# Layer norms moved into the stages around them, with their statistics taken block by block and a sqrt issued on ScalarE at a stage's end

## What is computed

```python
x = x + softmax_attention(_layernorm(x))
x = x + spline_ffn(_layernorm(x))
x = x + retention(_layernorm(x))
x = x + spline_ffn(_layernorm(x))
x = x + linear_attention(_layernorm(x))
x = x + conv_attention_moe(_layernorm(x))
x = x + rwkv(_layernorm(x))
x = x + conv_attention_moe(_layernorm(x))
```

```python
y = _layernorm(x)                       # of the layer's input
h = conv3(_layernorm(y) * ln1_w + ln1_b)  # causal, 3 taps, per channel
y = y + softmax_attention(h)            # with rope, 16 heads of 8
y = y + moe(_layernorm(y) * ln2_w + ln2_b)  # 4 experts, top 1
x = x + y
```

## Time and profile before

| | us |
|---|---|
| median of 3 runs | 2646.72 (2646.5 to 2649.6) |
| the profiled execution, device time | 2643.61 |
| its span in the trace | 2641.8 |
| PE, DVE, ACT, POOL busy | 2139.3, 1833.2, 1376.9, 362.9 |
| mean granted PE clock | 0.915 of 2.4 GHz |

### The profile page before, as it was taken

How to read it: one execution, slowest core, us unless ns; L and a number is a source line. 1 busy time by engine, 2 the same in 40 slices (tenths; PEclk the granted TensorE clock), 3 DMA queues, 4 the chain that set the end, 5 groups by cost and what they waited for, 6 DMA issues and landing times. The chain is left out here.

```text
span 2641.8 us, 39751 instructions
## 1 busy us (share of the span) xinstructions
PE 2139.3 (81%) x13146; PEld 943.1 (36%) x13324; DVE 1833.2 (69%) x4630; ACT 1376.9 (52%) x1968; POOL 362.9 (14%) x608
## 2 busy tenths in 40 slices
PE   3689999946799736557999998998347999999898
PEld 2123332224344424422233323665222233322565
DVE  6688788656577766668878874334968888884433
ACT  3246666772599643333566666222533566667221
POOL 4000110010454304100001001000000001101000
PEclk8699999987899868769999999999669999999899
DMA  7501020001011000061011000000052010000000
GB/s 193 140 1 37 2 38 1 1 1 48 31 51 45 18 0 1 0 189 36 1 38 38 1 1 1 1 0 0 0 163 61 1 38 21 18 1 1 1 0 16
DMA packets 48073, 81.68 MB, mean 31 GB/s; under 512 B 6348, under 2 KB 37836, under 8 KB 47228
## 3 DMA queue, kind: packets, MB, share of 16 engines
q1 hardware_dynamic: 42408, 71.34, 10.7%
q0 software_dynamic: 2528, 5.65, 0.7%
q10 hardware_dynamic: 2976, 2.67, 0.4%
HBM read 56.18 MB, written 23.07 MB: 30 GB/s over the span
## 5 line engine op out<-in xcount | busy, mean ns | idle before, releaser
L854 ACT ACTIVATE probs<-score 128x1024 f32<-128x1024 f32 x960 | 825.5, 896 | 522.8 <-PE score L918 519.7
L976 DVE TENSOR_REDUCE max_part<-stat 128x1 f32<-128x512 f32 x1152 | 722.0, 683 | 113.0 <-PE stat L868 110.4
L931 PE MATMUL pv<-probs,v_ones 128*9 128x512 f32 (+3 forms) x3840 | 443.7, 534 | 2.2 <-issue 1.0
L973 DVE CUSTOM_DVE_ANT_0 masked_scores<-stat,mask_row 128x128 f32<-128x128 f32 (+3 forms) x768 | 343.1, 487 | 102.2 <-PE stat L868 98.9
L868 PE MATMUL stat<-first_group_k,first_group_q 128*128 128x512 bf16 (+3 forms) x924 | 293.2, 371 | 91.1 <-DVE max_part L976 37.1
L828 POOL TENSOR_SCALAR_AFFINE_SELECT probs<-probs 128x256 f32<-128x256 f32 x384 | 154.0, 406 | 1249.3 <-ACT probs L854 1245.9
L868 PE MATMUL stat<-group_k,group_q 128*128 128x512 bf16 (+3 forms) x933 | 281.2, 348 | 18.3 <-DVE max_part L976 9.8
L918 PE MATMUL score<-first_group_q,first_group_k 128*128 128x512 bf16 (+3 forms) x921 | 253.3, 355 | 14.7 <-DMA first_group_q<-row_max_turned 8.3
L918 PE MATMUL score<-group_q,group_k 128*128 128x512 bf16 (+3 forms) x915 | 244.8, 348 | 10.1 <-DMA group_q<-row_max_turned 3.5
L1952 ACT ACTIVATE gate<-gate_ps 128x512 f32<-128x512 f32 x128 | 76.4, 597 | 262.0 <-PE gate_ps L1927 262.0
L868 PEld LDWEIGHTS stat<-first_group_k,first_group_q 128*128 128x128 bf16 x960 | 94.0, 99 | 269.3 <-DVE max_part L976 123.4
(11 more groups left out here) (308 smaller groups left out, 2353.9 us busy)
## 6 DMA issues: line engine op xcount, KB each, us to landing
q_parts<-parts_t SPq DMA_DIRECT2D x40, 384.0 KB, 4.0
group_k<-k_parts SPq DMA_DIRECT2D x18, 384.0 KB
group_q<-q_parts SPq DMA_DIRECT2D x18, 384.0 KB
k_parts<-parts_t SPq DMA_DIRECT2D x16, 384.0 KB, 4.9
head_q<-q_parts SPq DMA_DIRECT2D x48, 96.0 KB
head_k<-k_parts SPq DMA_DIRECT2D x48, 96.0 KB
first_group_k<-k_parts SPq DMA_DIRECT2D x9, 384.0 KB
first_group_q<-q_parts SPq DMA_DIRECT2D x9, 384.0 KB
```

The lines of the kernel that those rows point to most:

```text
L854: nc.scalar.activation(probs[:, n % PSLOTS, :, 0:width], sc[hp][:, :, 0:width], ACT.Exp, scale=scale).then_inc(expd.sem, 1)
L931: last = nc.tensor.matmul(acc[32 * h:32 * h + D + 1, f:BANK], v9[:, kt, g * HG + h, :], probs[:, (2 * t + h // 2) % PSLOTS, h % 2, 0:BANK ...
L973: nc.vector.tensor_tensor_reduce(masked[:, at % 2, 0:width], ring[n % RBANKS][:, 0:width], w["mask_row"][:, BANK - width:BANK], 1.0, NEG, ...
L976: nc.vector.reduce_max(into, ring[n % RBANKS][:], AX.X).then_inc(stat_used.sem, 1)
```

## The change

Every `layer_norm` stage and both `conv_stage`s go. What they did is spread over the stage before and the stage behind.

- **Statistics.** `RowStats.follow` is called behind each block's add in `output_stage`, `spline_ffn_stage` and `rwkv_stage`; it takes the statistics of the block before and gathers those of the block before that. What is left comes behind the last add. `experts_stage` takes them in `block_stats`, inside its loop. Only the first norm, of the loaded input, takes them all at once, as before (`known=False`).
- **Norm.** `Norm.dve`, `Norm.act` and `Norm.turn` stand at the head of the stage that uses the norm. Of each block DVE now normalises three tiles and ACT one, and ACT copies all four transposed blocks. PE transposes blocks 0 and 1, and the others between its own matmuls.
- **Double norm.** The two norms of conv_attention_moe's input are one pass: the variance of a normalised row is var / (var + eps), so the second scale follows from the first variance. The result of the first norm, `y`, is written by ACT later in `qkv_stage` (`first_norm`). The convolution runs by block on DVE (`convolve`): two blocks in the norm, two in front of `prepare` of the loop.
- **A root at the end.** `load_roots` takes the square root of one column of zeros as ACT's last instruction of a stage; nothing reads it.
- `output_stage` writes one PSUM bank for each block and adds 512 columns in one DVE instruction (before 128). `project_stage` has four PSUM banks (before eight).
- `EARLY` is 2 instead of 3: ACT reads back the rows of block 1, SP those of block 0, and the attention stage loads blocks 2 and 3.
- POOL's add of a bias, or of `y`, to `X` now waits until all rows are normalised.

```diff
-EARLY = 3
+EARLY = 2
...
+class RowStats:
...
+    def take(self, q):
+        for i in range(QC * q, QC * q + QC):
+            ins = self.nc.vector.bn_stats(self.raw[:, i, :], self.src[:, i, :])
+        ins.then_inc(self.read.sem, 1)
+    def gather(self, dve, q):
+        dve.wait_ge(self.read.sem, self.read.at(q + 1))
+        for i in range(QC * q, QC * q + QC):
+            ins = self.nc.vector.bn_aggr(self.mv[:, i, :], self.raw[:, i, :])
+        ins.then_inc(self.ready.sem, 1)
...
+    def follow(self, dve, q, rows):
+        if q >= 1:
+            dve.wait_ge(rows.sem, rows.at(q))
+            self.take(q - 1)
+        if q >= 2:
+            self.gather(dve, q - 2)
+        if q == NQ - 1:
+            dve.wait_ge(rows.sem, rows.at(NQ))
+            self.take(NQ - 1)
+            self.gather(dve, NQ - 2)
+            self.gather(dve, NQ - 1)
...
+def load_roots(k, w):
+    k.nc.scalar.sqrt(w["root"][:], w["mask_row"][:, 0:1])
...
+class Norm:
...
+        if not self.known:
+            for i in range(NT):
+                ins = nc.vector.bn_stats(self.raw[:, i, :], self.src[:, i, :])
+            chain(ins)
+            for i in range(NT):
+                ins = nc.vector.bn_aggr(mv[:, i, :], self.raw[:, i, :])
+            chain(ins)
+        ins = nc.vector.tensor_scalar(std[:, 0], mv[:, :, 1], self.eps, None, ALU.add)
+        if self.twice:
+            chain(ins)
+            ins = nc.vector.scalar_tensor_tensor(std[:, 1], std[:, 0], self.eps, mv[:, :, 1], ALU.mult, ALU.add)
+        ins.then_inc(self.var_ready.sem, 1)
+        if between:
+            between()
...
+        dve.wait_ge(self.std_ready.sem, self.std_ready.at(1))
+        chain(nc.vector.reciprocal(rstd[:], std[:]))
+        nc.vector.scalar_tensor_tensor(self.shift[:], bcast(mv[:, :, 0], 1, self.N), -1.0, rstd[:], ALU.mult, ALU.mult).then_inc(self.scale_ready.sem, 1)
+        for n, q in enumerate(self.order):
+            for i in range(QC * q, QC * q + QC - 1):
+                ins = nc.vector.tensor_scalar(self.dst[:, i, :], self.src[:, i, :], mv[:, i, 0:1], rstd[:, self.N - 1, i:i + 1], ALU.subtract, ALU.mult)
...
+            ins.then_inc(self.dve_rows.sem, 1)
+            if hook:
+                hook(n)
+        self.steps = chain.n
+    def act_tile(self, out, which, i):
...
+        nc = self.nc
+        act.wait_ge(self.var_ready.sem, self.var_ready.at(1))
+        nc.scalar.sqrt(self.std[:], self.std[:]).then_inc(self.std_ready.sem, 1)
+        act.wait_ge(self.scale_ready.sem, self.scale_ready.at(1))
...
+        def row(n):
+            self.act_tile(self.dst, self.N - 1, QC * self.order[n] + QC - 1).then_inc(self.act_rows.sem, 1)
+        row(0)
+        for n, q in enumerate(self.order):
+            if n + 1 < NQ:
+                row(n + 1)
+            act.wait_ge(self.turned.sem, self.turned.at(n + 1))
+            out = self.dst_t[:, q * BANK:(q + 1) * BANK]
+            if self.affine is None:
+                ins = nc.scalar.copy(out, self.banks[n])
+            else:
+                ins = nc.scalar.activation(out, self.banks[n], ACT.Identity, bias=self.affine[1][:, 0:1], scale=self.affine[0][:, 0:1])
+            ins.then_inc(self.kept.sem, 1)
...
+    def first_norm(self, out, c):
+        for i in range(QC * c, QC * c + QC):
+            ins = self.act_tile(out, 0, i)
+        ins.then_inc(self.first_out.sem, 1)
...
+    def convolve(self, dve, q):
...
+        here = self.conv[:, at:at + BANK]
+        dve.wait_ge(self.kept.sem, self.kept.at(q + 1))
...
+        ins.then_inc(self.convolved.sem, 1)
...
+    def turn(self, pe, n):
+        q = self.order[n]
+        pe.wait_ge(self.dve_rows.sem, self.dve_rows.at(n + 1))
+        pe.wait_ge(self.act_rows.sem, self.act_rows.at(n + 1))
+        for i in range(QC):
+            ins = self.nc.tensor.transpose(self.banks[n][:, i * P:(i + 1) * P], self.dst[:, QC * q + i, :], self.w["ident"][:])
+        ins.then_inc(self.turned.sem, 1)
+    def wait(self, eng, n):
+        sig = self.kept if self.conv is None else self.convolved
+        eng.wait_ge(sig.sem, sig.at(n + 1))
...
                 for q in range(NQ):
                     for n in range(q * NP, q * NP + NP):
@@ -402,53 +482,68 @@
                 for n, (_, dst) in enumerate(units):
                     act.wait_ge(turned.sem, turned.at(n + 1))
                     nc.scalar.copy(dst, tp[:, n % 4, :]).then_inc(kept.sem, 1)
+                load_roots(k, w)
...
-                    nc.vector.tensor_tensor(x[:, i, :], out[:, i % 4, 0:C], x[:, i, :], ALU.add).then_inc(used.sem, 1)
+                for q in range(NQ):
+                    dve.wait_ge(ready.sem, ready.at(q + 1))
+                    tiles = x[:, QC * q:QC * q + QC, :]
+                    nc.vector.tensor_tensor(tiles, out[:, q, :].rearrange("p (i c) -> p i c", c=C), tiles, ALU.add).then_inc(used.sem, 1)
+                    stats.follow(dve, q, used)
...
+                    norm.wait(pe, c)
...
+                    if c == 1:
+                        norm.wait(pe, NQ - 1)
...
+                norm.turn(pe, 0)
+                norm.turn(pe, 1)
                 project(0)
+                norm.turn(pe, 2)
+                norm.turn(pe, 3)
                 project(1)
...
+                norm.act(act)
...
+                    if norm.twice:
+                        norm.first_norm(first_norm, n)
                 if rows:
-                    load_rows(act, EARLY - 1)
+                    load_rows(act, 1)
...
+                def conv_ahead(n):
+                    if norm.conv is not None and n >= 2:
+                        norm.convolve(dve, n - 2)
+                norm.dve(dve, hook=conv_ahead)
...
                 prepare(0, lambda: None)
                 for n in range(NQ):
+                    if norm.conv is not None and n + 2 < NQ:
+                        norm.convolve(dve, n + 2)
...
-                    if rows and 0 < c < EARLY:
-                        load_rows(sp, c - 1)
+                    if rows and c == 1:
+                        load_rows(sp, 0)
...
                     for half in range(2):
+                        norm.turn(pe, 2 * c + half)
+                    for half in range(2):
+                        norm.wait(pe, 2 * c + half)
...
+                norm.act(act)
...
+                load_roots(k, w)
             @block.gpsimd
             def _(pool):
+                norm.wait_read(pool)
                 nc.gpsimd.tensor_tensor(x[:], x[:], bcast(w["bout"][:], 1, NT), ALU.add).then_inc(biased.sem, 1)
...
+                norm.dve(dve)
...
+                norm.turn(pe, 0)
+                norm.turn(pe, 1)
...
+                        if n == 0:
+                            if q + 2 < NQ:
+                                norm.turn(pe, q + 2)
+                            norm.wait(pe, q)
...
                 nc.scalar.activation(wa[:, 0, :], w["wT"][:, 8, :], ACT.Copy, scale=w["mix"][:, 0:1]).then_inc(wa_ready.sem, 1)
+                norm.act(act)
                 nc.scalar.activation(wneg[:], w["decay"][:], ACT.Exp).then_inc(w_ready.sem, 1)
...
+                load_roots(k, w)
...
-                chain(nc.vector.tensor_scalar(om[:], w["mix"][:], -1.0, 1.0, ALU.mult, ALU.add))
-                for n in range(3):
-                    nc.vector.tensor_scalar(wb[:, n, :], w["wT"][:, 8 + n, :], om[:, n:n + 1], None, ALU.mult).then_inc(wb_ready.sem, 1)
+                    stats.follow(dve, q, added)
+                def mix_weights():
+                    chain(nc.vector.tensor_scalar(om[:], w["mix"][:], -1.0, 1.0, ALU.mult, ALU.add))
+                    for n in range(3):
+                        nc.vector.tensor_scalar(wb[:, n, :], w["wT"][:, 8 + n, :], om[:, n:n + 1], None, ALU.mult).then_inc(wb_ready.sem, 1)
+                norm.dve(dve, between=mix_weights)
...
+                norm.turn(pe, 0)
+                norm.turn(pe, 1)
                 for i in range(NT):
+                    if i % QC == 0:
+                        if i // QC + 2 < NQ:
+                            norm.turn(pe, i // QC + 2)
+                        norm.wait(pe, i // QC)
                     ins = nc.tensor.matmul(lp[:, i * E:(i + 1) * E], h_t[:, i * P:(i + 1) * P], w["router"][:], start=True, stop=True)
...
+                norm.wait_read(pool)
                 nc.gpsimd.tensor_tensor(x[:], x[:], y[:], ALU.add).then_inc(added.sem, 1)
...
+                norm.act(act)
...
+                load_roots(k, w)
...
+                norm.dve(dve)
...
+                    if e < 0:
+                        block_stats(n)
+                def block_stats(n):
+                    tiles = [n * QC - QC + s for s in range(QC)]
+                    dve.wait_ge(out_used.sem, out_used.at(n * (E * QC)))
+                    for i in tiles:
+                        xi = x[:, bass.ds(i, 1), :].rearrange("p o c -> p (o c)")
+                        ins = nc.vector.bn_stats(w["row_stats"][:, bass.ds(i, 1), :].rearrange("p o s -> p (o s)"), xi)
```

(8 more changed lines are left out.)

256 lines of the change are left out of this document (117 added, 139 removed).

## The result

The changed kernel took 2635.0 us (median of 6 runs, 2623.8 to 2637.0), the kernel before 2648.5 beside it; forecast were 2609.7 and a range from 2599 to 2621. The ratio is 0.9936 (95% interval 0.9923 to 0.9950): 17 us faster by the ratio (13.5 between the two medians), where 37 were forecast and 26 to 48 were the range. A second set gave 2629.8 against 2647.1, ratio 0.9927 (0.9910 to 0.9943). The profiled execution took 2623.8 us, 19.8 less than the profiled one before. It is the shortest of its kernel, so I take lengths of stretches from it, and not the total. The direction was right and the forecast more than twice too large.

What follows compares the result with a forecast made beforehand. Norms were taken as bound by latency: DVE, ACT and PE work in turn, none full, awaiting all 16 tiles. Terms summed to 37.05 us, taking the profiled 2643.6 to 2606.6 and the median 2646.7 to 2609.7; range 2599 to 2621.

Steps and rivals of the forecast that it cites:

- Roots: Norm roots and their table: cost 0, since `load_roots` puts the table load ahead of the eps operation.
- rival 3: Root's table loaded again at eps: 11 roots, up to 1.1 us each, 12 in all; gain 25, 2622; chance 0.07.
- Statistics: Behind a stage's last add: shorter wait to eps, gain about 1.15 us at spline 1, 3.15 at rwkv; last experts stage loses 1.2.
- Norm in the stage: At the head of the stage using it: PE's own work begins 3.6 us after eps starts instead of 6.6.
- Experts: Start of the two experts stages, up to the logits: gain 1.0 us each with statistics, 2.0 together.
- rival 2: Cold starts: PE at half clock behind every transpose; gain 29.5 us, kernel 2617; chance 0.22.
- Double norm to rope: Convolution layers, from first norm's eps to first rope instruction: 14.75 us instead of 27.67, gain 12.9.
- minus 3.5 (range 2.5 to 4): Convolution layers' DVE-bound loop: loss from two of four blocks' convolutions now inside it, 2 x 1.5 us and their waits.
- The read-back: Two early blocks: convolution layers' stage end gains 2.8 us (1.5 to 4); late attention reads lose 0.8 for both layers.
- The +0.8 of landing: Attention 1: a gain of 0.8 us from landing, part of that layer's 3.0.
- rwkv: Scan start 10.75 us after eps instead of 9.11: loses 1.65; with 3.15 from statistics, gains 1.5.
- rival 4: Slower: lower PE clock in the long attention loops; a mean fall of 0.02 gives 2656 us; chance 0.03.

Runs made afterwards that it cites:

- e4: Changed kernel without the four calls that issue an unread root at a stage's end: 2631.9 us, ratio 0.9942.
- e6: Changed kernel with three separate edits: rwkv's exponential moved, experts' turns before the logits, no statistics in the last experts stage: 2624.4 us, ratio 0.9915.
- e10: Changed kernel plus seven unread PE products around the start of each experts stage, to keep PE busy: 2625.1 us, ratio 0.9910.
- e3: Changed kernel with three early blocks read back again instead of two: 2627.1 us, ratio 0.9923.
- e5: On top of e2, all four turns before project(0) in the qkv stages, and blocks 0 and 1 convolved behind all rows: 2619.0 us, ratio 0.9894.
- e14: On top of e5, all four convolutions ahead of the first rope instruction, none in the loop: 2613.7 us, ratio 0.9868.
- e2: Changed kernel with one PE wait changed: before turning block 1 it awaits the copy of norm block 3, not its convolution: 2624.2 us, ratio 0.9913.
- e7: On top of e2, the first norm's output written by POOL instead of ACT: 2624.6 us, ratio 0.9919.
- e13: Kernel before with two early blocks instead of three, nothing else of the change: 2646.6 against 2647.9 us, ratio 0.9996.
- e8: Changed kernel with the attention stage's reads of blocks 2 and 3 issued behind the first row maxima's DMA: 2636.9 us, ratio 0.9962.
- e9: Changed kernel with block 2 read ahead of the first row maxima's DMA and block 3 behind it, on separate semaphores: 2631.8 us, ratio 0.9943.
- e6a: Part of e6: rwkv's decay exponential placed between the norm's second and third copy on ACT; all three edits together 2624.4 us.
- e6b: Part of e6: in the experts, all four turns before the router's logits, as in the kernel before; all three edits together 2624.4 us.

## Why the prediction was wrong, step by step

- **Roots: right.** No load stands behind an eps. Without `load_roots` the starts of six norms come 5.6 us later in all, where rival 3 said 12 at eleven (e4).
- **Statistics: right within 0.4 us.** t0 came 2.7 to 3.0 us behind the last add. At rwkv it came 1.64 behind, for 1.6. The unread statistics of the last stage were mis-sized: 1.45 for loop and end, measured 2.2 to 2.5 (ledger, e6).
- **Norm in the stage: right where PE's own first matmul was asked** (t0 + 3.54 and 3.65 for 3.6), the spline and the linear layer. Retention's early start of 4.9 us was down to 1.1 at its last projection (646.0 and 644.9); forecast 2.6, measured 1.4. What took it there I did not test. The granted clock over its projections was 0.94 before (615.3 to 646.0) and 0.86 after (610.4 to 644.9).
- **Experts: the step that failed is the clock.** I took 1.0 each and measured 0.1. The output stage and the statistics gave 0.9, more than I had counted, but the stretch from t0 to the gate product got 0.9 longer (12.52 for 11.65) where I had it shorter by about 0.5. I had worked rival 2, the cold start, through for seven other stages and not for the experts. The rows on which I judged it unlikely show that transposes may be followed by full clock, not that they are. Shown by e10, where at full clock the stretch is 4.4 us shorter, and by the two experts stages of e3, 9.41 and 12.51, with and without a stretch at full clock. The rule of the Trainium skill that I weighed, "TensorE: Matmul & The Clock Gate", "Part 4: PE-mode transpose", that transposes do not count as PE being busy, fits 1634 to 1645 (0.50 through transposes and logits). It does not fit the kernel before: at six of its 12 norms the granted clock rose to 1.00 between t0 + 4.8 and t0 + 6.1, when PE had done nothing but transposes since t0 + 2 (at the linear layer's, 983.1 for a t0 of 977.43). In e10 the clock stayed at 1.00 through the same transposes, behind products: there they did not bring it down. What decides whether it rises is not shown.
- **Double norm to rope: right** (13.1 and 12.8 for 12.9), and in part by luck: the steps that I gave add up to t0 + 14.2 and not 14.75, and `project(0)` started at t0 + 6.17, not 5.3. I had also missed what could be improved: ACT's order cost 2.8 us a layer (e5).
- **The loop: the step that failed is "minus 3.5 (range 2.5 to 4)".** Measured 7.2 and 7.4. Of these 4.2 are the two convolutions' own time on DVE (e14), 2.06 us for one block where I had taken 1.5, a quarter of the instructions over 2048 columns, and 1.6 the wait for the convolution in `turn(1)` (e2), which stands in the diff and which I did not cost: it needs the copies out of the banks and waits for `convolved`, and DVE comes to that behind rope. 1.4 us remain between e14's 29.53 and the 28.1 of before. The rows name a place: DVE stood idle for 1.87 us in front of the first second cut, where it had been 0.17, behind a projection that took PE 4.44 us (before 2.75) with the granted clock at 0.50 for 3.4 us. That the clock is the cause is not tested. ACT's `first_norm` made no difference in e7.
- **The read-back: the largest miss, 10 us.** The end of the stage was right (1.8, 3.1, 3.2 us for 1.9, 2.8, 2.8). I had put the reads behind it down at 0.8 for two layers. They cost 2.7, 3.5 and 3.9, since they stand in front of the first maxima's DMA, on the path to the first score. I had asked when the rows are used, and not what small transfer is queued behind them. The +0.8 of landing that the sum has for attention 1 stands on no row; there the first score lost 2.7. e3 and e13 show the two sides cancel, e8 and e9 that moving the reads back only moves the wait. Both signs that I had named for being wrong came, the stretched loop and a wait for read-backs, the latter in front of the first score and not of the maxima.
- **rwkv:** forecast a loss of 1.65 behind eps, measured 2.0. The direction and the cause (Exp behind the copies) were right (e6a). That the exponential follows its load at once was seen again: 1830.42 + 1.28, and the exponential at 1831.72. A drain of about 1380 ns behind the load, as the Trainium skill has it ("ScalarE: Activation LUTs", "What ACT_TABLE_LOAD costs"), does not show here either.
- **The rivals.** None alone was the case. Rival 2 named the right mechanism at other places; rival 4 did not occur: behind the first score the attention stages moved by +1.9, -3.5 and -0.5 us, inside their spread, and the mean granted clock was 0.918 (before 0.915). The range was too narrow because it held each term's own error, not a missed term. The misses of reads and loop make 17.6 us, and forecast and profiled pair lie 17.3 apart; the 1.9 us of the experts and the smaller misses were made up for by the attention's spread, which is luck.
- **The arithmetic.** 12.9 - 3.5 + 2.8 + 0.9 is 13.1 and not the 12.7 that stands for the second convolution layer; the sum would be 37.45.

## What to carry to other kernels

When a step is moved off the end of a stage, ask what it is then queued in front of: a small transfer on the critical path behind a large one pays for it, and moving the large one once more only changes who pays. Where work is interleaved to start one engine early, look at the engine that empties its results; all blocks' steps first, then the work, was better by 2.8 us in the convolution layers (and 0.3 worse in the experts, e6b), and an idle stretch of DVE in front of the loop took two convolutions for 0.4 us that cost 4.2 inside it. A wait on the last product of a chain, where an earlier link frees the buffer, is a cost that is found by reading each new wait in the diff.

## What the runs showed of the hardware

- PE's pause in front of a norm costs more than the pause. With unread products in it, the same transposes and logits ran at a granted clock of 1.00 and not 0.50, and the stage reached its first gate product in 8.1 us and not 12.5 (2.5 to 2.7 us net).
- A DMA of a few rows landed within 3.13 us of its issue behind one block's reads, and held PE up until 6.55 us after it behind two.
- The attention stages of one kernel's executions differ by up to 5 us (471.3 and 476.5 us for the same stage), in their first 50 us. The traces show PE's clock at half for 3.4 us from 34 us into the stage in the one, and for 10.2 us from 38 us in the other. Medians of the same kernel lay 5.2 us apart between two sets.
